# The first layer of a four-layer image network on 32x32 array tiles: product maps read in place, partial sums joined by a selection matmul

## The reference, cut to what matters

```python
unf = _unfold(x, 3, 1, 1)                       # [B, C*9, L]: the nine shifted images
xp4 = unf.reshape(B, C, 9, L).transpose(0, 1, 3, 2)
f1 = xp4                                        # 9 linear features a channel
f2 = einsum('bclp,bclq->bclpq', xp4, xp4)       # products of two taps,
f2 = f2 * keep * (1 / sqrt(45))                 # of which the 45 with p <= q are kept
out = f1 @ W1 + f2 @ W2                         # over channels and features, 32 outputs
out = out.reshape(B, 32, 32, 32) + bias         # the [L, 32] result read as [32, L]
```

## Time and profile before

| | us |
|---|---|
| median of 3 runs | 372.82 |
| lowest and highest run | 371.9, 374.68 |
| profiled execution: span from its first to its last instruction | 369.9 |
| TensorE, VectorE, ScalarE, POOL busy in the span | 311.3, 229.8, 173.0, 44.0 |

### The profile page before, as it was taken

How to read it: one execution, slowest core, us unless ns; L and a number is a source line. 1 busy time by engine, 2 the same in 40 slices (tenths; PEclk the granted TensorE clock), 3 DMA queues, 4 the chain that set the end, 5 groups by cost and what they waited for, 6 DMA issues and landing times.

```text
span 369.9 us, 5771 instructions
## 1 busy us (share of the span) xinstructions
PE 311.3 (84%) x2163; PEld 109.3 (30%) x2186; DVE 229.8 (62%) x494; ACT 173.0 (47%) x334; POOL 44.0 (12%) x44
## 2 busy tenths in 40 slices
PE   5599665688997556999999999999999799885994
PEld 1133111232342112333232323323232222333931
DVE  5980053834846662668786886777877221579945
ACT  2100000012335546978888787878878786300000
POOL 5000600400000000001010100101010102405100
PEclk9989966999999986999999999999999999998798
DMA  2799996000066953970000000000000000000001
GB/s 87 155 202 226 205 182 171 0 3 0 10 194 139 140 108 109 248 313 2 2 2 2 2 1 1 2 1 4 0 3 0 1 3 0 2 0 1 4 2 57
DMA packets 6283, 23.89 MB, mean 65 GB/s; under 512 B 1048, under 2 KB 1816, under 8 KB 5712
## 3 DMA queue, kind: packets, MB, share of 16 engines
q1 hardware_dynamic: 6000, 23.43, 26.3%
q0 software_dynamic: 256, 0.11, 0.2%
HBM read 11.59 MB, written 2.37 MB: 38 GB/s over the span
## 4 chain that ended last, share of the span: by engine, by line
PE 44%; DVE 10%; issue 5%; ACT 4%; another core or an unknown queue 0%; DVEq 0%; ACTq 0%
PE ps L1160 12%; PE ps L1178 12%; PE ps L1137 11%; DVE arena_a L461 3%; ACT arena_b L677 3%; PE ps L1290 2%; PE ps L1183 2%; PE ps L1233 2%; DVE mx L889 1%; PE ps L1250 1%; ACT relus L685 1%; DVE arena_a L965 1%; DVE sums L884 1%; PE ps L1298 1%; PE ps L1006 1%
## 5 line engine op out<-in xcount | busy, mean ns | idle before, releaser
L677 ACT ACTIVATE arena_b<-ps 128x512 f32<-128x512 f32 x232 | 125.2, 608 | 33.5 <-PE ps L1160 16.8
L1137 PE MATMUL ps<-arena_a 128*128 128x450 bf16 x256 | 86.1, 364 | 16.0 <-issue 11.5
L1160 PE MATMUL ps<-arena_a 128*128 128x512 bf16 x207 | 78.1, 386 | 1.0 <-ACT arena_b L677 0.4
L889 DVE TENSOR_REDUCE mx<-ps 128x1 f32<-128x450 f32 x120 | 69.2, 617 | 6.5 <-PE ps L1137 4.8
L884 DVE CUSTOM_DVE_ANT_0 sums<-ps,relus 128x450 bf16<-128x450 f32 x68 | 41.2, 625 | 40.5 <-PE ps L1137 31.1
L1178 PE MATMUL ps<-arena_b,vt 128*32 128x512 f32 x448 | 59.7, 605 | 0.7 <-ACT arena_b L677 0.7
L1160 PEld LDWEIGHTS ps<-arena_a 128*128 128x128 bf16 x224 | 21.6, 98 | 76.9 <-ACT arena_b L677 50.4
L685 ACT ACTIVATE relus<-ps 128x450 f32<-128x450 f32 x68 | 37.4, 556 | 11.0 <-PE ps L1137 10.9
L1006 PE MATMUL ps<-zeros 128*128 128x512 bf16 x109 | 29.0, 407 | 8.4 <-DMA xa<-x 3.5
L1137 PEld LDWEIGHTS ps<-arena_a 128*128 128x128 bf16 x256 | 23.8, 99 | 40.1 <-issue 10.7
L639 ACT ACTIVATE arena_b<-ps 96x386 f32<-96x386 f32 x3 | 1.5, 490 | 63.3 <-PE ps L1055 63.2
(11 more groups left out here) (131 smaller groups left out, 250.0 us busy)
## 6 DMA issues: line engine op xcount, KB each, us to landing
arena_b<-arena_a SPq DMA_DIRECT2D x12, 578.0 KB, 10.4
arena_b<-wmodes SPq DMA_DIRECT2D x1, 4096.0 KB, 22.0
arena_a<-k_scratch SPq DMA_DIRECT2D x3, 516.8 KB
arena_b<-arena_a SPq DMA_DIRECT2D x4, 306.0 KB, 5.6
arena_a<-q_scratch SPq DMA_DIRECT2D x3, 384.0 KB
arena_b<-arena_a SPq DMA_DIRECT2D x4, 272.0 KB, 5.0
k_scratch<-arena_b SPq DMA_DIRECT2D x3, 344.5 KB, 3.3
cst<-consts SPq DMA_DIRECT2D x1, 1029.0 KB, 11.1
```

Of the source, the lines that this page charges most:

```text
L677: nc.scalar.activation(probs[:, n % PRING, :], ps[:, SCORE_RING[n % len(SCORE_RING)], :], ACT.Exp).then_inc(expd, 1)
L889: nc.vector.tensor_reduce(mx[:, a, e:e + 1], bank, AX.X, ALU.max).then_inc(max_read, 1)
L1137: mm(ps[:, block_bank(i), 0:KHALF], qst[:, e, g, qt * P:(qt + 1) * P], kst[:, g, at:at + KHALF], start=True, stop=True).then_inc(max_score ...
L1160: last = mm(ps[:, bank, :], kst[:, g, t * P:(t + 1) * P], qst[:, e, g, :], start=True, stop=True)
```

## The change

The maps are no longer stacked. TensorE's array is addressed as sixteen tiles of 32x32. The row of tiles is the image (its 32 channels, in the partitions in which the maps are written), the column of tiles is one of (half of the image's columns, feature of a pair). For every one of 54 features, in 27 rounds of two, sixteen matmuls of 512 columns run: two halves, two features, four images. Image b accumulates in bank b; the 32 output rows of a column tile hold the partial sum of every second feature for one half. Only twelve product maps and the squares are written (to arena_b); linear features read xp. Then ScalarE and VectorE copy two banks each to l0p, and a matmul with a 0/1 matrix (`l0sum`, 128 rows by 32) adds the two feature sums of a half and puts image b's result to output rows 32b of bank 4 + e. VectorE reads the halves one after the other, with the statistics between.

The weights, 54 x 32 columns for each of the four images (repeated), come as an input of their own in two transfers, followed by all constants in one. The order of the waits on POOL changes: it fills rows 64 to 95 of the k part with ones once xp is written; the clearing of the q part and VectorE's two fills go. The score matmuls contract over 72 or 75 rows. The four groups of five keep_clock matmuls during the maps go too. In `score_tile` the matmuls of the rest block (L1165) are cut to S_ROWS in the same way.

```diff
-TILES = [
-    ([(LINEAR, (0, 0)), ((0, 0), (0, 0)), ((0, 1), (0, 0)), ((1, 0), (0, 0))],
-     [(py, px) for py in range(3) for px in range(3)]),
-    ([((1, 1), (0, 0)), ((1, -1), (0, 1)), ((2, 0), (0, 0)), ((0, 2), (0, 0))],
-     [(0, 0), (0, 1), (1, 0), (1, 1)]),
-    ([((1, 2), (0, 0)), ((1, -2), (0, 2)), ((2, 0), (0, 2)), ((0, 2), (2, 0))], [(0, 0), (1, 0)]),
-    ([((2, 1), (0, 0)), ((2, -1), (0, 1)), ((2, 2), (0, 0)), ((2, -2), (0, 2))], [(0, 0), (0, 1)]),
-]
-SLOTS_PER_TILE = P // C
-N_MAPS = SLOTS_PER_TILE * len(TILES)
+SQUARE = (0, 0)
+SHIFTS = [(0, 1), (1, 0), (1, 1), (1, -1), (0, 2), (2, 0), (1, 2), (1, -2), (2, 1), (2, -1), (2, 2), (2, -2)]
+MAPS = [LINEAR, SQUARE] + SHIFTS
+N_MAPS = len(MAPS) - 1
...
+FEATURES = [(m, py, px) for m, d in enumerate(MAPS) for py in range(3) for px in range(3) if tap_pair(d, py, px)]
 N_KEPT = 45
...
+N_EARLY = sum(m < 2 for m, _, _ in FEATURES)
+L0_ROUNDS = len(FEATURES) // 2
...
-        maps = arena_a[:, 0:N_MAPS * NP].rearrange("p (m n) -> p m n", n=NP)
+        maps = arena_b[:, 0:N_MAPS * NP].rearrange("p (m n) -> p m n", n=NP)
+        l0w = arena_a[:, 0:N_L0W].rearrange("p (f o) -> p f o", o=32)
+        l0p = arena_b[:, 8192:8192 + B * HALF].rearrange("p (b n) -> p b n", b=B)
+        l0t = arena_b[:, 8192 + B * HALF:8192 + B * HALF + HW]
...
-            sp.dma_start(cst[:, 0:N_FIRST], consts[:, 0:N_FIRST]).then_inc(first_loaded, 16)
-            def stack_tile(t, n0, n1, signal):
-                maps_ = slice(SLOTS_PER_TILE * t, SLOTS_PER_TILE * (t + 1))
-                for b in range(B):
-                    sp.dma_start(stack[:, t % 3, b, n0:n1], maps[32 * b:32 * b + 32, maps_, n0:n1]
-                                 ).then_inc(signal, 16)
-            for cut, signal in enumerate((tile0_top, tile_in[0])):
-                sp.wait_ge(act_map, 2 * cut + 2)
-                sp.wait_ge(map_ready, 2 * cut + 2)
-                stack_tile(0, *CUTS[cut], signal)
-            for t in range(1, len(TILES)):
-                sp.wait_ge(map_ready, SLOTS_PER_TILE * (t + 1))
-                if t == 3:
-                    sp.wait_ge(tile0_used, 1)
-                stack_tile(t, 0, NP, tile_in[t])
-            sp.dma_start(cst[:, N_FIRST:N_CONST], consts[:, N_FIRST:N_CONST]).then_inc(consts_loaded, 16)
+            at = N_EARLY * 32
+            sp.dma_start(arena_a[:, 0:at], l0weights[:, 0:at]).then_inc(l0w_loaded[0], 16)
+            sp.dma_start(arena_a[:, at:N_L0W], l0weights[:, at:N_L0W]).then_inc(l0w_loaded[1], 16)
+            sp.dma_start(cst[:], consts).then_inc(consts_loaded, 16)
...
-            sp.wait_ge(q_filled, 1)
...
-            pool.wait_ge(tile0_top, B * 16)
-            for t in range(2):
-                pool.wait_ge(tile_in[t], B * 16)
-            nc.gpsimd.memset(arena_a[64:P, 0:q_words], 0.0).then_inc(q_filled, 1)
-            pool.wait_ge(q_filled, 1)
+            pool.wait_ge(padded, 1)
+            nc.gpsimd.memset(arena_a[64:96, q_words:q_words + k_words], TWO_ONES).then_inc(k_filled, 1)
+            pool.wait_ge(k_filled, 1)
             pool.wait_ge(l0_done, 1)
             nc.gpsimd.memset(xst[:], 0.0).then_inc(xst_zeroed, 1)
             pool.wait_ge(xst_zeroed, 1)
-            pool.wait_ge(k_filled, 2)
-            nc.gpsimd.memset(kst[64:P, :, KEYS:KPAD], 0.0).then_inc(k_padded, 1)
+            nc.gpsimd.memset(kst[64:96, :, KEYS:KPAD], 0.0).then_inc(k_padded, 1)
             pool.wait_ge(k_padded, 1)
-            pool.wait_ge(l0_read, 2)
+            pool.wait_ge(l0_read, 4)
...
-            for n0, n1 in CUTS:
-                nc.scalar.activation(maps[:, 0, n0:n1], xp[:, n0:n1], ACT.Copy).then_inc(act_map, 1)
-                nc.scalar.activation(maps[:, 1, n0:n1], xp[:, n0:n1], ACT.Square, scale=VOLTERRA_SCALE ** 0.5
-                                     ).then_inc(act_map, 1)
+            nc.scalar.activation(maps[:, 0, :], xp[:, 0:NP], ACT.Square, scale=VOLTERRA_SCALE ** 0.5
+                                 ).then_inc(act_map, 1)
             act.wait_ge(l0_done, 1)
+            for b in (0, 2):
+                nc.scalar.activation(l0p[:, b, :], ps[:, b, :], ACT.Copy).then_inc(l0p_act, 1)
...
-            order = [(SLOTS_PER_TILE * t + i, d, sy * WP + sx) for t, (maps_, _) in enumerate(TILES)
-                     for i, (d, (sy, sx)) in enumerate(maps_)]
-            steps = [(n0, n1, *step) for n0, n1 in CUTS for step in order[2:4]]
-            steps += [(0, NP, *step) for step in order[4:]]
-            for n0, n1, m, (dy, dx), pre in steps:
-                at = dy * WP + dx + pre
-                nc.vector.scalar_tensor_tensor(maps[:, m, n0:n1], xp[:, pre + n0:pre + n1], VOLTERRA_SCALE,
-                                               xp[:, at + n0:at + n1], ALU.mult, ALU.mult).then_inc(map_ready, 1)
-            dve.wait_ge(tile0_top, B * 16)
-            last_tile = (N_MAPS - 4) * NP
-            for t, (w0, w1) in ((2, (q_words, last_tile)), (3, (last_tile, q_words + k_words))):
-                for tile in range(t + 1):
-                    dve.wait_ge(tile_in[tile], B * 16)
-                nc.vector.memset(arena_a[64:P, w0:w1], TWO_ONES).then_inc(k_filled, 1)
+            for m, (dy, dx) in enumerate(SHIFTS):
+                n = NP - dy * WP
+                at = dy * WP + dx
+                nc.vector.scalar_tensor_tensor(maps[:, 1 + m, 0:n], xp[:, 0:n], VOLTERRA_SCALE,
+                                               xp[:, at:at + n], ALU.mult, ALU.mult).then_inc(map_ready, 1)
             dve.wait_ge(l0_done, 1)
-            dve.wait_ge(first_loaded, 16)
-            l0t = stack[:, 2, 0, 0:HW]
-            nc.vector.transpose(l0t.rearrange("p (j o) -> p j o", o=32),
-                                banks(0).rearrange("p (i j) -> p j i", j=32)).then_inc(l0_read, 1)
-            dve.wait_ge(l0_read, 1)
-            nc.vector.scalar_tensor_tensor(xb[:], l0t, c_("l0bias"), xa[:], ALU.add, ALU.add).then_inc(l0_read, 1)
-            dve.wait_ge(l0_read, 2)
-            dve.wait_ge(act_map, 4)
-            norm(xb[:], interior(xp)).then_inc(padded, 1)
+            for b in (1, 3):
+                nc.vector.tensor_copy(l0p[:, b, :], ps[:, b, :]).then_inc(l0p_dve, 1)
+            dve.wait_ge(consts_loaded, 16)
+            for e in range(2):
+                half = slice(e * HALF, (e + 1) * HALF)
+                dve.wait_ge(l0_summed, e + 1)
+                nc.vector.transpose(l0t[:, half].rearrange("p (j o) -> p j o", o=32),
+                                    ps[:, 4 + e, :].rearrange("p (i j) -> p j i", j=16)).then_inc(l0_read, 1)
+                dve.wait_ge(l0_read, 2 * e + 1)
+                nc.vector.scalar_tensor_tensor(xb[:, half], l0t[:, half], c_("l0bias"), xa[:, half], ALU.add, ALU.add
+                                               ).then_inc(l0_read, 1)
+                dve.wait_ge(l0_read, 2 * e + 2)
+                link(nc.vector.bn_stats(stats[:, 6 * e:6 * e + 6], xb[:, half]))
+            dve.wait_ge(act_map, 1)
+            norm_from_stats(xb[:], interior(xp)).then_inc(padded, 1)
...
-            for n in (1, 3, 5, 6):
-                pe.wait_ge(map_ready, n)
-                keep_clock(7, 5)
-            l0w = c_("l0w").rearrange("p (s o) -> p s o", o=32)
-            pe.wait_ge(first_loaded, 16)
+            pe.wait_ge(padded, 1)
+            pe.wait_ge(l0w_loaded[0], 16)
+            for r in range(L0_ROUNDS):
+                pair = FEATURES[2 * r:2 * r + 2]
+                newest = max(m for m, _, _ in pair)
+                if r > 0 and newest > max(m for m, _, _ in FEATURES[0:2 * r]):
+                    if newest == 1:
+                        pe.wait_ge(act_map, 1)
+                    else:
+                        if newest == 2:
+                            pe.wait_ge(l0w_loaded[1], 16)
+                        pe.wait_ge(map_ready, newest - 1)
+                for e in range(2):
+                    for i, (m, py, px) in enumerate(pair):
+                        column = slice(32 * (2 * e + i), 32 * (2 * e + i) + 32)
+                        for b in range(B):
+                            row = slice(32 * b, 32 * b + 32)
+                            image = maps[row, m - 1, :] if m else xp[row, :]
+                            last = mm(ps[column, b, :].rearrange("p (y x) -> p y x", x=W // 2), l0w[row, 2 * r + i, :],
+                                      window(image, py, px + 16 * e, 0, H, W // 2), start=(r == 0),
+                                      stop=(r == L0_ROUNDS - 1), skip_group_check=True)
+            last.then_inc(l0_done, 1)
+            pe.wait_ge(consts_loaded, 16)
+            l0sum = c_("l0sum").rearrange("p (e o) -> p e o", e=2)
             for e in range(2):
-                rows = [slice(32 * b, 32 * b + 32) for b in range(B)]
-                for s, (t, (py, px)) in enumerate(SLOTS):
-                    if t == 0:
-                        if s == 0:
-                            pe.wait_ge(tile_in[0] if e else tile0_top, B * 16)
```

(41 more changed lines are left out.)

48 lines of the change are left out of this document (14 added, 34 removed).

## The result

The changed kernel takes 349.56 us in the median of four runs (346.56 to 351.5) against 373.06 for the kernel before in the same comparison: ratio 0.9382 [0.9337, 0.9426]. It is faster by 6.2%, inside the range and 7.9 us above the predicted 341.7. The run that was profiled was the slowest of the four: 351.5, with a span of 349.4.

A forecast was written before the change was run, and what follows sets the result against it. The prediction took the first layer to live on transfers; normalisation 31.1 us earlier cuts the 369.9 us span to 338.8, plus 2.9 for launch and end gives 341.7 us. Own range 338.2 to 345.5, reaching to 353.5 over rivals.

The forecast's parts named there:

- (a): First layer: weights come late, each of 54 passes shows a 0.109 us load, + 5.9, 347.6 us; chance 0.13.
- (b): First layer: load and matmul pairs are issued at 40 ns each, + 11.6, 353.3 us; chance 0.09.
- When the layer can begin, what hides beside it: First layer's matmuls start at 8.7 us; weights, constants and maps arrive before they are wanted, 7 us in the tightest place.
- If the sixteen run side by side as the four do now, a round costs the same 0.86 us: First layer: 27 rounds of sixteen matmuls at 0.86 us make 23.2 us, so the layer ends at 32.1.
- Eight loads side by side at 18.78: Old first layer: eight weight loads within 0.23 us, taken as evidence that loads run beside matmuls.
- 29.6 ns a pair: First layer: issue rate of load and matmul pairs, 0.95 us a round, 2.4 us too much over 27 rounds as upper end.
- (c): First layer: only two row groups run together or the clock stays low, doubling the round, + 23.2, 364.9 us; chance 0.06.
- (d): First layer: four images' writes to the same output partitions take turns, 3.44 us a round, + 69.7, 411 us; chance 0.04.
- (e): First layer: a row group's four loads wait for its matmuls and stand one behind another, + 23.5, 365.2 us; chance 0.03.
- Behind the layer: Copies, selection matmuls, transpose, bias and statistics after the first layer: 6.6 us, normalisation of layer 2 starting at 38.7.
- The score matmuls read 75 and 72 rows where they read 128. I take nothing: Score stage: fewer rows counted as no change in time, with 1 us kept to either side.
- What the first layer gains goes to the end one for one: All later stages: each waits for the one before, so the 31.1 us earlier normalisation reaches the end whole.

The follow-up runs named there:

- e4: The changed kernel with every first-layer matmul streaming 256 columns instead of 512, result incomplete; 350.22 us in one run.
- e6: The changed kernel with every first-layer matmul streaming 128 columns instead of 512, result incomplete; 340.83 us in one run.
- e9: The changed kernel run again, unaltered; median 349.74 us of six runs, ratio 0.938 to the kernel before.
- e10: The changed kernel with all 128 rows back in the block-maximum and score matmuls; median 346.06 us of six runs, ratio 0.9281 to the kernel before.

## Why the prediction held in its direction and fell short by 8 us

**The range.** The 349.56 lies outside the forecast's own 338.2 to 345.5 (whose upper end adds up to 344.9 from the terms that it names). It lies inside the stated range because that reached over rivals (a) and (b), and (a), at 347.6, is the one that came.

**What bounds the kernel.** Held. The layer was set by its transfers; without them it ends at 37.54 us, before at 65.12.

**When the layer can begin, what hides beside it.** Held: start 8.56 (forecast 8.7), POOL's memset 9.30 us as estimated, maps finished at 23.4 (23.7), TensorE without a gap, DMA share 0.05 in the layer. The constants landed near 10.4 (issued at 2.59, 7.8 us to landing) and not at 24.5; being hidden either way, this changed nothing.

**"If the sixteen run side by side as the four do now, a round costs the same 0.86 us".** This step failed. The round was 1.07, the layer 28.98 in place of 23.4: 5.6 us, the largest part of the miss. It is the price of rival (a), one load of 0.11 in each of 54 passes, to which I gave 0.13: its step of 0.539 was measured as 28.98 / 54 = 0.537. Eight loads side by side at 18.78, my evidence against it, said something of four tiles and nothing of sixteen. Of the 29.6 ns a pair, my upper bound for the forecast, the reading was wrong as well: pairs follow each other at 18.4 ns in e4 and 13.5 in e6, and the floor is one of supply, 3.6 to 3.8 us for 128 pairs. By this floor sixteen tiles at 0.86 a round, 3.44 us for 128 pairs, could not have been kept up through the layer either. (b), (c), (d) and (e) didn't occur; their rounds of 1.29 to 3.44 were seen nowhere.

**Behind the layer.** 7.07 us where 6.6 was forecast (37.54 to 44.61): right but for 0.5.

**"The score matmuls read 75 and 72 rows where they read 128. I take nothing".** Wrong by its kind. I compared durations at one clock, and there the rows cost next to nothing, 0.5 us in 145. What they change is how long the lower clock is granted once it has fallen. Together this is 3.3 us in the profiles from the first score to the end (231.07 against 227.73), 3.7 in the medians of e9 and e10. That exceeds the 1 us that I kept to either side; the 1.6 that I kept for spells placed anew was not tied to the rows.

**"What the first layer gains goes to the end one for one".** True up to the 24 one-column matmuls (25.16, then 25.56). Then the first block maximum came 6.45 us after the first of these where the old one came after 4.80; TensorE stood still for q's landing just before it for 3.20 us, in the old kernel for 1.55. From the one to the other it is 4.02 to 6.45 us in the profiles of the change and of the variants with its whole layer, and 4.73 (1.48 of standing still) in e9, the same kernel, so these 1.65 are scatter. The rest is the row count above.

**The sum.** 338.8 was forecast for the span and 349.4 came: 5.6 for the rounds less 0.1 for the earlier start, 0.5 behind the layer, 0.4 regained up to the one-column matmuls, 1.6 at the q stop, 0.1 up to the score, 3.3 behind it. Of these 10.6 us, 1.9 is that the profiled run lay above its median; 0.8 comes off since the time is 1.9 to 2.3 above the span in every run here, and not 2.9: the remainder that I called launch held 0.8 of scatter. 10.6 - 1.9 - 0.8 = 7.9.
